# A top-1 expert stage of a graph network layer: gathers, weight loads and cleaning in another order, and a first layer of 492 columns

## The reference

```python
C = max(1, math.ceil(1.25 * T / E))            # T = 3125 tokens, E = 8 experts: C = 489
x = h.reshape(T, D)                            # D = 256
probs = softmax(x @ gate_w + gate_b)
idx = argmax(probs);  prb = probs[idx]         # one expert a token
pos = (cumsum(one_hot) * one_hot).sum(-1) - 1  # its place in the expert's queue
kept = pos < C
buf = zeros((E, C, D)).at[idx, pos].set(x, mode='drop')
hmid = relu(einsum('ecd,edf->ecf', buf, w1) + b1[:, None, :])   # F = 1024
ybuf = einsum('ecf,efd->ecd', hmid, w2) + b2[:, None, :]
y = nan_to_num(ybuf[idx, min(pos, C - 1)] * (prb * kept)[:, None], nan=0, posinf=1e4, neginf=-1e4)
```

## Time and profile before

| | |
|---|---|
| runs | 2595.56, 2594.28, 2591.94 us; median 2594.28 |
| the profiled execution | 2593.7 us |
| its span in the profile | 2592.0 us |
| mean granted clock of PE | 0.929 of full speed |
| PE busy | 2263.9 us (87% of the span) |
| DVE busy | 1988.8 us (77%) |
| POOL busy | 1553.1 us (60%) |
| ACT busy | 1438.7 us (56%) |
| the eight experts on PE | 872.63 to 1139.55 us of the span |

### The profile page before, as it was taken

One profiled execution on the slowest core, in us unless ns is written; L12 is line 12 of the kernel. 1 busy time (PEld: TensorE's weight loads), 2 busy tenths in 40 slices (PEclk: granted clock), 3 DMA queues, 4 the chain that ended last, 5 costly groups with the idle time before them and its releaser, 6 DMA issues. The chain is left out here.

```text
span 2592.0 us, 61390 instructions
## 1 busy us (share of the span) xinstructions
PE 2263.9 (87%) x16596; PEld 1882.5 (73%) x16596; DVE 1988.8 (77%) x7341; ACT 1438.7 (56%) x4584; POOL 1553.1 (60%) x1544
## 2 busy tenths in 40 slices
PE   5785878999887699877999999999999998848993
PEld 3674546886663456545899999999999998728993
DVE  8885799999886535246899999999999998574334
ACT  0882003444442122226788888888888887623441
POOL 1236777777773577424777777777777774505541
PEclk9897588999997799989999999999999999869997
DMA  5313333443434244412333333333333333052224
GB/s 179 111 31 101 103 95 98 104 103 101 105 103 145 65 148 148 159 49 77 90 78 80 79 79 79 79 79 78 79 78 79 89 77 69 8 197 74 70 69 166
DMA packets 245577, 246.34 MB, mean 95 GB/s; under 512 B 142916, under 2 KB 202335, under 8 KB 244996
## 3 DMA queue, kind: packets, MB, share of 16 engines
q0 software_dynamic: 57344, 151.11, 21.3%
q1 hardware_dynamic: 184596, 88.07, 12.4%
q10 hardware_dynamic: 3312, 3.28, 0.4%
HBM read 189.82 MB, written 52.50 MB: 93 GB/s over the span
## 5 line engine op out<-in xcount | busy, mean ns | idle before, releaser
L2355 POOL DMA_INDIRECT l_rows<-xl_tab,l_ra x454 | 453.3, 998 | 138.7 <-issue 99.4
L1030 POOL DMA_INDIRECT room_a<-h_tab,c_rec x432 | 439.8, 1018 | 138.7 <-issue 80.5
L1077 PE MATMUL c_ps<-room_a 128*128 128x256 f32 x864 | 311.3, 450 | 83.5 <-DVE room_a L1359 48.0
L2363 POOL TENSOR_TENSOR l_low<-l_rest 128x520 bf16<-128x520 f32 x227 | 239.4, 1055 | 134.9 <-DVE l_rest L2509 133.0
L1047 ACT ACTIVATE s_cum<-iota_f,c_row_f 128x128 f32<-128x128 f32 x391 | 122.8, 389 | 313.0 <-PE c_ps_s L1115 206.6
L1077 PEld LDWEIGHTS c_ps<-room_a 128*128 128x128 f32 x864 | 161.5, 211 | 183.4 <-DVE room_a L1359 127.2
L2402 ACT ACTIVATE l_val<-l_rows,l_val 128x64 f32<-128x64 f32 x908 | 241.7, 337 | 7.4
L2392 ACT ACTIVATE room_a<-room_a,l_cexp x908 | 241.4, 345 | 1.2 <-issue 1.0
L2427 PE MATMUL l_bank_l<-g_att_d,l_rz 128*128 128x4 f32 x1816 | 240.6, 253 | 1.1 <-ACT l_rz L2414 0.9
L2471 PE MATMUL l_ps_lb<-ident,l_ls 128*128 128x128 f32 x1816 | 235.3, 273 | 0.4 <-DVE l_ls L2533 0.3
L1115 PE MATMUL c_ps_s<-s_cum 128*128 128x272 f32 x782 | 230.3, 392 | 0.0
(11 more groups left out here) (631 smaller groups left out, 6067.5 us busy)
## 6 DMA issues: line engine op xcount, KB each, us to landing
m_w<-in_L_ffn_w SPq DMA_DIRECT2D x16, 1024.0 KB, 8.1
rec_a<-room_a SPq DMA_DIRECT2D x114, 102.0 KB
l_ra<-rec_a SPq DMA_DIRECT2D x227, 51.0 KB, 2.4
e_w<-in_L_ffn_W SPq DMA_DIRECT2D x16, 512.0 KB, 12.2
l_rows<-xl_tab,l_ra POOLq DMA_INDIRECT x454
room_a<-h_tab,c_rec POOLq DMA_INDIRECT x432, 2.8
e_w<-ye_buf SPq DMA_DIRECT2D x4, 1280.0 KB, 11.0
yd_buf<-m_clean SPq DMA_DIRECT2D x7, 512.0 KB, 4.0
```

Source lines behind the costliest of these rows:

```text
L1030: pool.indirect_dma_start(rows[:, u, :], None, K["h_tab"], bass.IndirectOffsetOnAxis(ap=rec[:, n % RSLOTS, k, 0:1].bitcast(I32), axis=0)). ...
L1077: pe.matmul(ps[s % NB][:, :], hot[:, u, :], rows[:, s % RU, :], start=True, stop=True).then_inc(s_agg, 1)
L2355: pool.indirect_dma_start(rows[:, u, j, :], None, K["xl_tab"], bass.IndirectOffsetOnAxis(ap=ra[:, u, j, A_SRC:A_SRC + 1].bitcast(I32), axi ...
L2363: pool.tensor_tensor(low[:, r % 2, :], rest[:, r % 2, :], uppers(rest[:, r % 2, :]), ALU.subtract).then_inc(S["low"], 1)
```

## The change

Four engines' programs get another order, and the first layer is narrower:

- POOL issues gather(n + 2) ahead of the wait for part n and its scatters, not behind them.
- SP stores expert s-3 in round s, not s-2, and the 17 loads stand in round 6, not 4.
- DVE cleans earlier: expert 0 ahead of part 3, experts 1 and 2 ahead of part 4, expert 3 ahead of part 5.
- ACT waits for the cleaning of each group of expert s-2 ahead of that group's eviction, not for all of them ahead of the first.
- The first layer's matmuls and relu evictions have CAPM = 492 columns in place of 512. The transposes and the copies into `xint` still have 512. The columns 492 to 511 of `hid`, which the second layer still reads, are set to zero once, by a memset on DVE ahead of the reduction that yields the tokens' weights.

```diff
+CAPM = -(-CAP0 // 4) * 4
@@ sync: for s in range(EXP0)
-                if s >= 2:
-                    store(s - 2)
-                if s == 4:
+                if s >= 3:
+                    store(s - 3)
+                if s == 6:
                     sp.wait_ge(s_staged, PARTS_A)
@@ sync: after the loop
+            store(EXP0 - 3)
             store(EXP0 - 2)
@@ gpsimd
             for n in range(PARTS_A):
+                gather(n + 2)
                 pool.wait_ge(s_staged, n + 1)
...
-                gather(n + 2)
@@ scalar
-                    act.activation(hid[:, f, :], ps_h[f % 2][:, :], ACT.Relu,
+                    act.activation(hid[:, f, 0:CAPM], ps_h[f % 2][:, 0:CAPM], ACT.Relu,
...
-                wait(act, s_clean, NQ * (s - 1))
                 for q in range(NQ):
                     act.wait_ge(s_yp, NQ * s + q + 1)
+                    if s >= 2:
+                        act.wait_ge(s_clean, NQ * (s - 2) + q + 1)
@@ tensor
-                        mm = pe.matmul(ps_h[f % 2][:, :], w1[:, u, k, f * P:(f + 1) * P], xint[:, k, :],
+                        mm = pe.matmul(ps_h[f % 2][:, 0:CAPM], w1[:, u, k, f * P:(f + 1) * P], xint[:, k, 0:CAPM],
@@ vector
             dve.wait_ge(s_wt, 1)
+            o.did(dve.memset(hid[:, :, CAPM:CAPR], 0.0))
+            o.then()
             dve.tensor_reduce(weight[:, :], ps_share.rearrange("p f q -> p q f"), AX.X, ALU.add).then_inc(s_wcol, 1)
@@ vector, the order
-            for n in range(4):
+            for n in range(3):
                 staged(n)
             cleaned(0)
+            staged(3)
+            cleaned(1)
+            cleaned(2)
             staged(4)
-            cleaned(1)
+            cleaned(3)
             staged(5)
-            cleaned(2)
-            cleaned(3)
             cleaned(4)
             linear_parts()
             edge_weights()
```

## The result

The changed kernel took 2569.2 us, the median of four runs from 2561.3 to 2576.8, beside 2594.07 for the kernel before: a ratio of 0.9905, with a 95% interval from 0.9888 to 0.9921. The prediction was 2566.3, between 2563 and 2576. Over all 18 runs that I have of it the median is 2568.3, and over all 47 of the kernel before 2595.3.

A forecast was written before the change was run, and what follows sets the result against it. PE was taken to bound the kernel, held up in the expert stage by late rows, weights and the slowed clock. Savings of 23.72 + 4.3 = 28.0 us gave 2566.3 us, range 2563 to 2576 (its own 2563 to 2571).

The forecast's parts named there:

- The waits, 15.70: Expert stage: PE's waits on gathered rows (4.55, 2.06 us) and weights (9.09 us) all go, 15.70 us.
- The slow clock inside the stage, 8.02: Experts 2 to 5: the 8.02 us that PE loses to the halved clock around its waits comes back.
- e0's 2.67: Expert 0's excess of 2.67 us over an undisturbed expert stays, because PE is idle before it either way.
- Columns, 4.3: First-layer matmuls: time goes with columns, so 20 fewer save 4.3 us over eight experts.
- The stage, 28.0: Whole expert stage, 266.92 us before: waits, slow clock and narrower columns together save 28.0 us.
- The stages behind do the same work after the same barrier: nothing: After the expert stage: time to the kernel's end unchanged at 1452.5 us; a difference over 2 makes the prediction wrong.
- DVE's order: DVE in the expert stage: earlier cleaning fits into its idle time, 93.8 us for scatters alone; no separate saving.
- The finer s_clean waits are met 40 us early. Nothing.: ACT's evictions in the expert stage: waiting for cleaning group by group changes no time.
- SP queue: SP in the expert stage: weights issued 29.5 us before use, so the 9.09 us wait at expert 5 goes.
- Rival A: First-layer matmuls: columns don't pay, something else paces them; time 2570.6 us, chance 0.05.
- Rival B: Expert stage: a PE wait on late rows or weights stays; 2569 to 2572, up to 2578.5 us, chance 0.13.
- Rival C: Expert stage: slower, as a late store delays cleaning, scatters, gathers, then PE in a ring; 2594 to 2600 us, chance 0.04.

The follow-up runs named there:

- e5: Not a run: the sixth of the eight experts that PE works through in the expert stage, counted from zero; 32.87 us start to start in the kernel before.

## Why the prediction was right, point by point

**The waits, 15.70: right.** None is left, in any of the four profiles. The suppliers came where the steps had put them: cleaned(0) began at 923.94 (predicted "at about 927"), staged(3) at 949.63 (949), staged(5) at 1020.50 (1020), the last gather's issue ended at 1056.4 (1055.7). edge_weights ended at 1052.6 (1052).

**The slow clock inside the stage, 8.02: right.** All of it came back with the waits. The table shows the reverse too: an undisturbed stage is 238.8 us with 492 columns and 243.1 with 512, and each kernel with waits is longer than that by its waits and 2.9 to 8.1 us more. The prediction's "Elsewhere the granted clock stays 1.00" was read off one window of 50 us, and it does not: the trace of before has stretches of 17.1 and 10.2 us at half clock behind the stage too. e0's 2.67 stayed, at 32.20 - 29.52 = 2.68.

**Columns, 4.3: right in the stage.** A first layer went from 13.74 to 13.20, 0.54 an expert. At the medians 2.2 and 3.0 arrived, and their intervals don't exclude 4.3. An estimate from the Trainium skill's figures for a sustained stream (TensorE: Matmul & The Clock Gate, Back-to-back issue gap) gave 1.3 us in all. The rows say 4.3, so for these fp32 matmuls the trace decides against that estimate.

**The stage, 28.0: right.** From 266.92 it came down to between 238.58 and 238.98 in four profiles, by 27.9 to 28.3. The memset took 0.19 us (0.2).

**"The stages behind do the same work after the same barrier: nothing": the step that failed.** The same work does not take the same time. In four profiles of one kernel it took 1452.55 to 1463.4 us, and nearly all of the difference lies between the stage's end and the attention's first aggregation, where the clock goes down in a gap and comes back sooner or later. The profile of before had fallen at the low end, 1452.45; all profiles but the first of the change lie between 1452.2 and 1457.5, those of two kernels with the old orders of the other engines among them (1457.46 and 1454.32). The prediction called itself wrong if this time differed by over 2 us from 1452.5. It did in three profiles of four, by 10.9, 3.6 and 3.8, and the fourth is within 0.1: the sign was drawn from one profile and could not tell this change from chance.

The forecast of the time was less wrong than that. The change took 24.9, 28.3, 26.9 and 28.1 us less than the median of the kernel before beside it, 27.0 over all runs, where the sum had 28.0. The first set, by which the forecast is held to 2569.2, happened to give the smallest gain of the four. The forecast's own range, 2563 to 2571, was too narrow: single runs reach 2561.3 and 2576.8. The 1.8 either way rested on three runs.

**DVE's order: right in sign, not priced.** The prediction said why DVE can afford to clean early. Of what late cleaning costs it had only one path, through stores and weights on the SP queue; its sentence on gather(7) speaks of DVE without idle time. With DVE's old order and all the rest new, no weights and no gather were late. ACT waits for the cleaning of the expert two before, since `yout` has two buffers, and PE waits for ACT, 6.28 us. The sentence "The finer s_clean waits are met 40 us early. Nothing." holds only under the new order of DVE, and even there the four groups of experts 0 and 1 are cleaned only 24 to 33 us ahead of their evictions.

**SP queue: right, and larger than the 9.09 and 2.82 of before suggest.** Once the other waits are gone, PE reaches the weights of e5 earlier and the same queue costs 26.4. Its 17 loads took 14.7 us to issue (1025.28 to 1039.96), not 9.5; nobody waited for that.

**Rival A** fell by the 4% shorter first layer. **Rival B** fell in every profile; the slowest landing of gathered rows was 7.0 to 8.8 us in the four profiles of the change and not 6.7, still inside the 9.3 that the margin allowed. **Rival C** did not occur with all parts in. A chain like it does show with POOL's part alone, from scatters through cleaning, stores and weights to PE, and that kernel is slower than before by 0.3%; but it has the old orders of SP and DVE, so it doesn't show the rival's own ring.

**What stays open.** What fixes where the clock falls behind the stage is not settled, nor is it shown that the clock makes the difference there and doesn't only go along with it: the time follows the time at half clock in seven profiles without throwaway work, but the two with it had less of that ahead of the first aggregation, 23.9 and 27.3 us, and reached it no sooner, 116.1 and 117.0 us after the stage's end. The last three profiles of the change were taken on three chips, which may be part of it; but on one chip single runs of it differ by up to 11.3 us. Also open is why runs with 492 columns spread over 2.7 to 15.5 us in a set of four or five and those with 512 in the new order over 1.5 and 1.7.

## What to carry to other kernels

Where several suppliers feed one engine, list each one's delivery time against the time at which it will be wanted under the new schedule, and change all those that come late together. One part tried alone can show nothing or a loss, though the whole gives 1%. And take the time of untouched stages from several executions: a single profile can lie 11 us from the next.

## What the runs showed that I had not expected

- The same code behind the stage took 1452.55, 1456.08, 1456.3 and 1463.4 us. The loop of the attention took 940.6 to 941.8 in every profile; nearly all of the spread is ahead of it, where PE goes between idle and busy.
- Filling PE's gaps with throwaway matmuls shortened the stretch at the low clock from 17.1 to 6.8 us and gained nothing: the first 5.4 of the fillers' own 7.59 us ran at that clock, and the work behind them started no earlier.
- A wait of a few microseconds on PE can cost more than itself: in the kernel with DVE's old order 6.28 us of waits came with some 4.5 us more, most of it slower matmuls. Not every wait does: the 2.62 us for the rows of e3 in the kernel without POOL's part cost only 0.2 more (e2 took 32.37 from start to start, not 29.52).
